# A selective-scan kernel in float32 on Trainium2: the convolution's bias moved from ScalarE to TensorE, and the second pass of the sigmoid left out

## The reference

```python
def _causal_conv_silu(x, w, b):
    k = w.shape[-1]
    y = conv_general_dilated(x, w, padding=[(k - 1, 0)], feature_group_count=x.shape[1])
    return jax.nn.silu(y + b[None, :, None])
...
u = _causal_conv_silu(x, conv_w, conv_b)
x_dbl = jnp.einsum('bdl,kd->bkl', u, xproj_w)
...
delta = jax.nn.softplus(delta + dt_bias[None, :, None])
dA = jnp.exp(jnp.einsum('bdl,dn->bdln', delta, A))
dBx = jnp.einsum('bdl,bnl,bdl->bdln', delta, Bm, u)
h = _ssm_scan(dA, dBx)
y = jnp.einsum('bdln,bnl->bdl', h, Cm)
y = y + Dp[None, :, None] * u
return y * jax.nn.silu(z)
```

## Time and profile before

| | |
|---|---|
| time, median of 3 runs | 818.29 us (816.92 to 818.44) |
| time of the profiled execution | 815.69 us |
| its span, first to last instruction | 813.9 us |
| busy in the span | PE 727.0, DVE 738.6, ACT 740.7, POOL 698.0 us |
| mean granted clock of TensorE | 0.973 of full speed |

### The profile page before, as it was taken

One profiled execution on the slowest core, in us unless ns is written; L12 is line 12 of the kernel. 1 busy time (PEld: TensorE's weight loads), 2 busy tenths in 40 slices (PEclk: granted clock), 3 DMA queues, 4 the chain that ended last, 5 costly groups with the idle time before them and its releaser, 6 DMA issues. The chain is left out here.

```text
span 813.9 us, 11948 instructions
## 1 busy us (share of the span) xinstructions
PE 727.0 (89%) x3921; PEld 376.6 (46%) x3921; DVE 738.6 (91%) x800; ACT 740.7 (91%) x1423; POOL 698.0 (86%) x339
## 2 busy tenths in 40 slices
PE   7877999889998899989999899998999889998995
PEld 5435354353634436353453536444363444635363
DVE  4667899989999899998999989998999989999996
ACT  3699999999999999999989999899999999899890
POOL 0288789897998979899898979989798997989995
PEclk9798999999999999999999999999999999999698
DMA  6547072441806136070631608144180804417000
GB/s 198 147 118 144 1 170 54 104 95 41 173 24 162 37 86 151 26 173 1 150 88 59 140 4 194 40 116 82 57 180 4 188 7 119 106 42 155 2 14 26
DMA packets 55117, 74.80 MB, mean 92 GB/s; under 512 B 6784, under 2 KB 23568, under 8 KB 55056
## 3 DMA queue, kind: packets, MB, share of 16 engines
q1 hardware_dynamic: 54624, 73.79, 38.8%
q10 hardware_dynamic: 432, 0.26, 0.1%
HBM read 62.49 MB, written 11.53 MB: 91 GB/s over the span
## 5 line engine op out<-in xcount | busy, mean ns | idle before, releaser
L697 POOL TENSOR_TENSOR hst<-hst,c_rep 128x1024 f32<-128x1024 f32 x255 | 596.5, 2369 | 71.6 <-DVE hst L593 54.8
L593 DVE TENSOR_TENSOR_SCAN hst<-da,b_ps 128x512 f32<-128x512 f32 x512 | 580.4, 1198 | 28.9 <-issue 13.8
L408 ACT ACTIVATE da<-rep,neg_a 128x511 f32<-128x511 f32 x504 | 330.7, 709 | 3.5 <-DVE hst L593 3.1
L395 ACT ACTIVATE dbx_t<-du_t,b_t 128x256 f32<-128x256 f32 x640 | 274.1, 496 | 4.7 <-PE b_ps L910 4.0
L910 PE MATMUL b_ps<-ident,dbx_t 128*128 128x128 f32 x1536 | 224.0, 284 | 55.7 <-DVE hst L593 37.8
L910 PEld LDWEIGHTS b_ps<-ident,dbx_t 128*128 128x128 f32 x1536 | 173.1, 144 | 161.0 <-DVE hst L593 87.8
L933 PE MATMUL y<-hst,sum_sel 128*32 128x512 f32 x1024 | 138.9, 616 | 0.0
L814 PE MATMUL pb<-xnt,conv_wt 128*128 128x512 f32 x240 | 110.5, 603 | 13.8 <-ACT du_t L378 13.0
L888 PE MATMUL b_ps<-du,spread_sel 32*128 32x512 f32 x256 | 89.4, 669 | 0.5 <-DVE hst L593 0.4
L582 DVE TENSOR_TENSOR b_ps<-b_ps,b_rep 128x1024 f32<-128x1024 f32 x64 | 77.8, 1218 | 9.5 <-PE b_ps L888 6.0
L814 PEld LDWEIGHTS pb<-xnt,conv_wt 128*128 128x128 f32 x240 | 43.1, 189 | 80.8 <-issue 61.1
(11 more groups left out here) (120 smaller groups left out, 457.4 us busy)
## 6 DMA issues: line engine op xcount, KB each, us to landing
rep<-d_scr SPq DMA_DIRECT2D x128, 256.0 KB, 9.5
c_rep<-bc_scr SPq DMA_DIRECT2D x64, 256.0 KB, 4.9
d_scr<-t_pos SPq DMA_DIRECT2D x16, 512.0 KB, 3.0
b_rep<-bc_scr SPq DMA_DIRECT2D x64, 64.0 KB, 2.3
x_ln<-x SPq DMA_DIRECT2D x8, 256.0 KB, 3.8
x_res<-x SPq DMA_DIRECT2D x8, 256.0 KB, 3.1
out<-x_res SPq DMA_DIRECT2D x8, 256.0 KB, 2.3
rep<-x SPq DMA_DIRECT2D x7, 256.0 KB, 4.7
```

Of the source, the lines that this page charges most:

```text
L395: ins = nc.scalar.activation(dbx_t[(NX * d + q - 1) % 2][:, c, :, r, :], du_t[d][:, c, :, :], ACT.Copy, scale=b_t[d][:, c, n:n + 1])
L408: nc.scalar.activation(da[s % 2][:, j, 1:L], rep[d][h][:, j, 1:L], ACT.Exp, scale=neg_a[:, d, h, j, q:q + 1]).then_inc(decay_done, 1)
L593: nc.vector.tensor_tensor_scan(hst[s % RING][:, j, :], da[s % 2][:, j, :], b_ps[:, j, :], 0.0, ALU.mult, ALU.add).then_inc(scan_done, 1)
L697: nc.gpsimd.tensor_tensor(hst[s % RING][:, two, :], hst[s % RING][:, two, :], c_rep[d][:, q:q + 1, :].broadcast_to([P, 2, L]), ALU.mult).t ...
```

## The change

1. The bias is loaded as a row (`bias_w`, one partition of 128, the others zero), and each `conv` begins with one more matmul of that row by a tile of ones. The bank then holds convolution plus bias.
2. ACT's tanh loses its bias operand, and the second pass is gone.
3. DVE makes (tanh + 1) times the bank, which is twice u. The factor 2 is taken out in `xproj` and `skip` (halved once on DVE in the prologue), in the copy of `du`'s transposes (scale 0.5 in L378's instruction), and in `spread_sel` (halved on the host).
4. `spread_sel` also serves the replicas of `t_pos`, which are not doubled; there the matmul is issued twice into the same bank, so that the halves add up.
5. PE waits in the prologue for the bias row and the ones; POOL writes two more tiles; SP issues one more DMA.

```diff
             def u_sigmoid(d, V, h):
                 act.wait_ge(conv_filled, 2 * V + h + 1)
                 wait(act, u_ready, 2 * V)
                 source = y[:, h, :] if V == 1 else pb[:, 1 - h, :]
-                nc.scalar.activation(t_exp[:, h, :], source, ACT.Tanh, bias=half_bias[:, d, h:h + 1], scale=0.5).then_inc(u_step, 1)
-                act.wait_ge(u_step, 2 * V + h + 1)
-                nc.scalar.activation(t_exp[:, h, :], t_exp[:, h, :], ACT.Copy, bias=0.5, scale=0.5).then_inc(u_sig, 1)
+                nc.scalar.activation(t_exp[:, h, :], source, ACT.Tanh, scale=0.5).then_inc(u_sig, 1)
...
-                nc.vector.scalar_tensor_tensor(u[d][:, h, :], source, col[:, d, 0, h:h + 1], t_exp[:, h, :], ALU.add, ALU.mult).then_inc(u_ready, 1)
+                nc.vector.scalar_tensor_tensor(u[d][:, h, :], t_exp[:, h, :], 1.0, source, ALU.add, ALU.mult).then_inc(u_ready, 1)
...
             def conv(d, V, h, taps, free, count):
                 wait(pe, free, count)
                 bank = y[:, h, :] if V == 1 else pb[:, 1 - h, :]
+                if 0 in taps:
+                    mm(bank, bias_w[:, d, P * h:P * (h + 1)], ones[:, :], start=True, stop=False)
                 for k in taps:
...
-                    ins = mm(bank, conv_wt[d][:, k, P * h:P * (h + 1)], window, start=k == 0, stop=k == TAPS - 1)
+                    ins = mm(bank, conv_wt[d][:, k, P * h:P * (h + 1)], window, start=False, stop=k == TAPS - 1)
...
-                    mm(pb[:, j % 2, :], spread_sel[at, :], t_pos[at, h, :], start=True, stop=True).then_inc(rep_filled, 1)
+                    mm(pb[:, j % 2, :], spread_sel[at, :], t_pos[at, h, :], start=True, stop=False)
+                    mm(pb[:, j % 2, :], spread_sel[at, :], t_pos[at, h, :], start=False, stop=True).then_inc(rep_filled, 1)
...
-            nc.vector.tensor_scalar(half_bias[:, :, :], col[:, :, 0, :], 0.5, None, ALU.mult).then_inc(weights_ready, 1)
+            for d in range(2):
+                nc.vector.tensor_scalar(xproj[d][:, :, :, :], xproj[d][:, :, :, :], 0.5, None, ALU.mult).then_inc(weights_ready, 1)
```

More of the change, by code:

```diff
@@ L33, with build @@
 SKIP_AT = 3
-def build(nc, x, win_t, wz_t, conv_w, cols, xproj_t, dt_t, a_log, wout_t, ffn_w, had, ident_d, sum_sel_d, spread_d, out):
+def build(nc, x, win_t, wz_t, conv_w, bias_rows, cols, xproj_t, dt_t, a_log, wout_t, ffn_w, had, ident_d, sum_sel_d, spread_d, out):
     ctx = ExitStack()
@@ L50, in build @@
         col = sb("col", [P, 2, 3, NH])
-        half_bias = sb("half_bias", [P, 2, NH])
+        bias_w = sb("bias_w", [P, 2, DI])
+        ones = sb("ones", [P, L])
         xproj = [sb(f"xproj{d}", [P, NH, 2, XC]) for d in range(2)]
@@ L106, in build @@
         conv_loaded = sem("conv_loaded")
+        bias_loaded = sem("bias_loaded")
+        ones_ready = sem("ones_ready")
         zeroed = sem("zeroed")
@@ L139, in build @@
         conv_filled = sem("conv_filled")
-        u_step = sem("u_step")
         u_sig = sem("u_sig")
@@ L249, in _ @@
             sp.dma_start(spread_sel[:, :], spread_d).then_inc(w_loaded, DMA)
-            sp.wait_ge(zeroed, 8)
+            sp.wait_ge(zeroed, 9)
+            sp.dma_start(bias_w[0:1, :, :], bias_rows).then_inc(bias_loaded, DMA)
             for d in range(2):
@@ L378, in keep_dut @@
                 nc.scalar.activation(du_t[d][:, 2 * n:2 * n + 2, :, :],
-                                     pb[:, 1 - n, :].rearrange("p (c j e) -> p c j e", c=2, j=NH * NJ), ACT.Copy).then_inc(dut_ready, 1)
+                                     pb[:, 1 - n, :].rearrange("p (c j e) -> p c j e", c=2, j=NH * NJ), ACT.Copy, scale=0.5).then_inc(dut_ready, 1)
             def z_sigmoid(b):
@@ L415, in _ @@
             nc.scalar.activation(neg_a[:, :, :, :, :], neg_a[:, :, :, :, :], ACT.Exp).then_inc(a_exp, 1)
-            act.wait_ge(weights_ready, 5)
+            act.wait_ge(weights_ready, 6)
             u_sigmoid(0, 0, 0)
@@ L618, in _ @@
                 for h in range(NH):
-                    nc.vector.tensor_scalar(skip[:, d, h, :], ident[:, :], col[:, d, 2, h:h + 1], None, ALU.mult).then_inc(set_step, 1)
+                    nc.vector.tensor_scalar(skip[:, d, h, :], ident[:, :], col[:, d, 2, h:h + 1], 0.5, ALU.mult, ALU.mult).then_inc(set_step, 1)
             nc.vector.tensor_scalar(wout[:, :, :], wout[:, :, :], 0.5, None, ALU.mult).then_inc(weights_ready, 1)
@@ L753, in _ @@
             pool.wait_ge(const_ready, 3)
+            nc.gpsimd.memset(bias_w[:, :, :], 0.0).then_inc(zeroed, 1)
+            nc.gpsimd.memset(ones[:, :], 1.0).then_inc(ones_ready, 1)
             for d in range(2):
@@ L938, in _ @@
             warm(16)
-            pe.wait_ge(zeroed, 8)
+            pe.wait_ge(zeroed, 9)
+            pe.wait_ge(bias_loaded, DMA)
+            pe.wait_ge(ones_ready, 1)
             transpose_xn(0, first_xn, 1)
@@ L948, in _ @@
             pe.wait_ge(w_loaded, DMA * W_LOADS)
-            pe.wait_ge(weights_ready, 5)
+            pe.wait_ge(weights_ready, 6)
             x_proj(0, 0)
@@ L1073, in constants @@
     sum_sel = np.tile(np.eye(CB, dtype=np.float32), (NR, 1))
-    return had, ident, sum_sel, np.ascontiguousarray(np.tile(sum_sel.T, (NJ, 1)))
+    return had, ident, sum_sel, np.ascontiguousarray(0.5 * np.tile(sum_sel.T, (NJ, 1)))
 def kernel(**inputs):
@@ L1093 @@
         "conv_w": np.stack([v[s[0]][:, 0, :].T for s in sides]),
+        "bias_rows": np.stack([v[s[1]] for s in sides])[None],
         "cols": np.stack([np.stack([halves(v[s[n]]) for n in (1, 4, 6)], 1) for s in sides], 1),
```

## The result

| | before | after |
|---|---|---|
| time, median of 20 runs each | 816.67 us (815.54 to 818.57) | 819.44 us (818.05 to 820.91) |
| ratio | | 1.0034, 95% interval 1.0025 to 1.0043 |
| profiled execution: time, span | 815.69, 813.9 us | 819.11, 817.3 us |

The change makes the kernel 2.8 us slower. Part of that is the base: the three runs shown beforehand had a median of 818.29, twenty have 816.67. (Of these twenty, 14 lie at 815.5 to 816.9 and 6 at 818.3 to 818.6; the profiles are of the first kind, so they show a loss of 3.4 us where the medians show 2.8.) The larger part is the size of one term, as the profile shows.

The account below looks back on a forecast made before the run. No single engine was taken as the bound; all four are nearly full in the loop. Terms 1.95 (x_proj), 4.7 (replicas), -0.1 (u) and 0.7 (loop) sum to 7.25 us, giving 825.6 us, stated range 820 to 831.

Parts of the forecast that it names:

- What bounds the kernel: Loop: four nearly full engines, no single bound; a saving counts only where another engine stands still for it.
- those 1.6 us: Loop: DVE's two waits for the sigmoid per batch; the second pass could at best give back part of them.
- Prices: Per-instruction costs: bias matmul 0.87 us; tanh without bias 580 ns; DVE's instruction for u 671 ns against 747.
- The loop: Seven batches: forward unit -0.1 us, backward unit +0.2, so +0.1 a batch and +0.7 in all.
- Rival B: Loop: the matmul's 0.87 us stays once in each of 14 units, 12.2 us in all; 837.1 us, chance 0.11.
- D: Loop: bias matmul lies in PE's waits, the sigmoid's waits vanish, DVE keeps 1.6 us a batch; 813.6 us, chance 0.05.
- x_proj: Prologue: its start moves from 20.69 to 22.65 us behind the bias matmuls, +1.95 us.
- The replicas: Prologue: doubled matmuls lengthen ACT's four pairs by 0.4, 0.9, 1.7 and 1.7 us, the last two at clock 0.50; +4.7.
- Rival A: Prologue: the clock stays high during the replicas, so they cost 1.1 us in place of 4.7; 822.0 us, chance 0.20.
- The fourth bias matmul: Prologue, behind the copies: beside DVE's first scans, given nothing, or 0.87 us if that cover is gone.
- C, strict order: Prologue: a pair's eight records run in turn, costing 13.9 us in place of 4.7; 834.8 us, chance 0.04.

Follow-up runs that it names:

- the matmul by zeros: The kernel before with one more matmul by zeros ahead of each half of the convolution, all else as it was: 830.23 us, ratio 1.0164.
- the gain alone: The changed kernel without the bias matmul, so the bias is left out of the computation: 801.73 us, ratio 0.9811 to the kernel before.

## Why the prediction was wrong

**What bounds the kernel** was right in the main, and the waits were mapped onto the right instructions. The limit that the second pass can "at best" give back a part of those 1.6 us was too low: without the bias matmul a batch is 2.08 shorter.

**Prices.** 0.87 for the bias matmul: shown (half 0's start to the inputs behind it took 4.36 us in the change, 3.51 before, 0.85 more). The Trainium skill ("FP8 and Floating Point Precision", TensorE Precision Notes) has true fp32 as four passes of the array; at 2.4 GHz that is 4 × 512 / 2.4 = 0.85 us as an estimate, and the trace agrees (0.85). Tanh 0.58 became 0.59, u 0.67 became 0.68.

**The loop**, forecast +0.7 us over seven batches: measured 0.0, with a batch 0.09 longer in steady state (forecast 0.1); that the whole comes to nothing is luck, by the 0.6 us that the first batches gained. Its mechanism, 0.87 lost at slot 7 and made good before u, stands in the trace row by row. Rival B, that it stays, is refuted by the equal loops; the matmul by zeros shows that it would have stayed (+12.3 us) had the sigmoid not become shorter. D was refuted too: of PE's two waits the one ahead of half 0 stands as it was (0.86 us, 0.85 before), and the one of 1.01 ahead of half 1 is used up, mostly by half 0's longer convolution; half 1 starts 8.69 us behind half 0 where it started 8.91 behind, 0.2 earlier as forecast. My first estimate of the gain alone was off, 15 us and not 7 to 9.

**x_proj**, forecast +1.95: 1.78. The bias row's DMA and the two tiles of POOL, taken as hidden, were: the first convolution starts at 11.12 and 11.35 us in the two profiles of the change, at 11.27 and 11.00 before.

**The replicas are the step that failed: "Sum +4.7", for which "the third and fourth lie in the stretch 29.8 to 40 with a granted clock of 0.50".** Its mechanism is right (the doubled matmuls lengthen the turns of PE and ACT, and that passes on), its size is not. From ACT's first pair to PE's first transpose it takes 39.44 − 29.77 = 9.67 us where it took 9.17, and the first pair itself is 0.3 later than x_proj's shift explains: 0.8 in this profile in place of 4.7, and 2.6 in the second by the same reckoning. A turn with doubled replicas at the upper clock takes 2.75 us, about as long as one with single replicas at the lower (2.85). I took the clock of a fixed stretch of the old trace as given, though the edit changes what TensorE does in it. In the six profiles with doubled replicas the fall came 3 to 10 us later than in the six with single ones. Rival A had this, with 0.20 where it deserved more.

**But A was not all of it.** Its own argument for the low chance, that the kind of work is the same, is refuted by the six profiles. Its size, 1.1 us, fits the first profile (0.8), not the second (2.6) and not the timed runs: 2.2 us by the medians of the change with and without doubling, 2.0 to 3.0 in the kernel before. A late fall slows what stands behind the replicas: in the first profile the transposes start 2.58 us later than before, and DVE's multiplication behind the copies 2.88.

**The fourth bias matmul**, given nothing "and 0.87 if that cover is gone": between 43.46 and 54.63 the shift grows from 2.88 to 3.43, with DVE waiting 0.55 for u. The convolution there began at the lower clock, which lasted until 45.67, and this is what took the cover away. With single replicas the same bias matmul stands there, the clock is back at 41.85, and u waits for nothing; with doubled replicas and no bias matmul u waits 0.41. How much of the 0.55 is the bias matmul's is not separated.

**The sum by the profile** is 1.78 + 0.8 + 0.3 + 0.55 = 3.43 us in place of 7.25 (x_proj, the replicas, the copies behind them at the lower clock, the wait for u).

**C, strict order:** refuted. The pairs of doubled replicas are 2.75 us apart, and their eight records take 28.71 + 1.07 − 27.75 = 2.03 us where in turn they would take 3.5. The code issues L901 and L902 for one tile and then L901 and L902 for the next, yet in the trace all four records of L901 start (27.75 to 28.33) before the first of L902 (28.71): the second tile's first matmul starts ahead of the first tile's second. So the statement that every engine's instructions keep the code's order is too strong for PE: here two matmuls on different rows did not start in it. The Trainium skill's sentence on order ("TensorE: Matmul & The Clock Gate", The mechanism), read over whole matmuls in program order, does not hold for these. The bias's records among those of the copies show the interleaving too, though there the whole matmuls start and end in order.

**The base:** 1.6 of the 6.2 us between forecast and measurement are that 818.29 was a high sample of the kernel before.

## What to carry to other kernels

When an edit gives work from one engine to another, price both halves alone at each place: here two edits of 12 and 15 us cancelled, and the visible result came from the prologue, where about half of it was a side effect of taking out the factor 2. A wait of the busiest engine is worth something only if no later wait of it hangs on another engine's chain; follow that chain before moving anything. A granted clock is part of what an edit changes: do not carry the clock of an old stretch over to new work in it. And a matmul that uses few rows is cheap beside matmuls on other rows (0.65 us less here) and not elsewhere: in the prologue it cost 0.3 us more than the one on all rows.

## What the runs showed of the hardware

TensorE's clock fell from 2.4 to 1.2 GHz while the engine was busy. This is the kernel before, ahead of the fall at 29.82:

```profile
26.00:29.82 3.82, 3.47 (x16) 1.69 (x16) 1.57 (x3) 3.05 (x6) 3.58 (x10) 1.00 0.62 187
```

PE was busy 3.47 of these 3.82 us, with replicas and copies on 32 rows each and short waits for ACT (0.35 the longest), and in the slow stretch behind it 9.31 of 10.20. Twice the replicas, still on 32 rows, kept the upper level 3 to 10 us longer. The lower level lasted 10.2 to 13.7 us with single replicas and 6.8 to 10.2 with doubled ones. What in that work decides it, these runs don't tell.

Two fp32 matmuls of 32x512 on different rows took 1.17 us together and four of them 2.03, their records interleaved, where one of 128x512 took 0.85 to 0.87.
